# Cross attention and quantised FFN on one core: exponentials head by head from the score bank, a written-out start, and both barriers rebuilt

## Chip, cores, metric

One Trainium2 chip, one of its cores. The metric is the device time of one execution in microseconds; less is better. Times of a kernel come from several runs, and one further execution is profiled.

## What is computed

Eight batches of 512 rows with 512 columns. The first half is a cross attention against 77 context rows per batch with 8 heads, the second half an FFN with activations and weights rounded to 8-bit integers, where the activation's scale comes from the maximum of the whole tensor.

```python
x = x + _L0_xattn_ref(_layernorm(x), ctx_768, Wq, Wk, Wv, Wo, bo)
x = x + _L0_ffn_ref(_layernorm(x), clip_x, clip_down, w_gate, w_up, w_down)

# attention
attn = jnp.einsum('bhsd,bhld->bhsl', q, k) * scale
attn = jax.nn.softmax(attn, axis=-1)
out = jnp.einsum('bhsl,bhld->bhsd', attn, v)

# FFN
def _act_fake_quant(x, clip_factor):
    scale = jax.nn.sigmoid(clip_factor) * jnp.max(jnp.abs(x)) / QMAX
    return jnp.clip(_ste_round(x / scale), -QMAX - 1.0, QMAX) * scale
xq = _act_fake_quant(x, clip_x[0])
gate = xq @ wq(w_gate).T ; up = xq @ wq(w_up).T
h = _act_fake_quant(silu(gate) * up, clip_down[0])
return h @ wq(w_down).T
```

(The last four lines are shortened; wq stands for the weights' rounding, one scale per row.)

## The kernel before

Every instruction is recorded by hand into one queue per engine (class Chain, lines 6 to 60): `add(engine, fn, waits, sig)` appends an instruction that waits for the tokens in `waits` and counts up the semaphore `sig`. Each engine runs its queue strictly in the order in which the Python code calls `add`; nothing else sets the order. PE is TensorE, DVE VectorE, ACT ScalarE, POOL GpSimd; DMAs are issued from SP.

The 4096 rows are 32 row tiles of 128, four per batch. PSUM has QO (two banks, for products of queries, values and attention outputs), SP (two banks, the scores of one row tile: heads 0 to 3 in one, 4 to 7 in the other), PTP (two banks, transposed probabilities), WOP and MI (output products). Products of fp32 precision are three matmuls on a high and a low half: `xT_hi`, `xT_lo` and the like are the splits, one copy on ACT and one subtraction on DVE or POOL.

Per row tile n the attention does: `S(n)`, the score product (line 464), into SP; `soft_max(n)`, a maximum per head on DVE (477); `soft_sub(n)`, scores minus maximum into SBUF, on DVE (484); `soft_exp(n)`, one exponential over all 616 values on ACT, its scale being the row's layer norm factor `r8` (488); `soft_sum`, `soft_rec` on DVE (494, 497); `soft_norm` on POOL (505); `PT(n)`, transposes on PE (517), and `PT_high`, `PT_low`, which copy them out on ACT and DVE. `S(n)` may overwrite the bank once the subtraction of tile n-1 has read it: its waiting list names `t_sub.get(n - 1)`. Per batch come four `q_chunk(b, m)` (the queries, twelve matmuls each, copied out by ACT), `PV_rest` and four `PV` (probabilities times values, 552 to 562, copied out through `os_` by ACT and DVE), and per tile `wo(n)`, the output product (582 to 584, twelve matmuls). `residual`, `second_stats`, `second_scale`, `normed` and `largest` make the second layer norm and its maximum; `w_load` to `w_integer` round one weight tile per step.

`attend(s)` writes out step s. It treats tile s's transposes and tile s+1's scores, in four forms by t = s % 4, and the first batch has exceptions of its own in it. On PE a step with t=0 ends with `PT(s)`, `S(s+1)`; t=1 is `q_chunk`, `S(s+1)`, `wo`, `PT(s)`; t=2 is `S(s+1)`, two `q_chunk`, `wo`, `PT(s)`; t=3 is `S(s+1)`, `wo`, `PT(s)`, `q_chunk`. Ahead of the loop stand value row products `v_rows(0)` to `(2)`, the others lie in the first steps. `last_batch()` writes out steps 28 to 31, where S(30) uses QO and S(31) waits for tile 29.

Between the halves stands the first barrier, `whole_scale(0, ...)` (lines 1053 to 1069): the maximum of all rows of the normed tensor per partition, a transpose on PE to one partition, maximum, scale and reciprocal on 1x1, a second product that spreads both over the partitions, and a copy. `keep_clock(n)` puts n idle products of 128x128 into PE's queue. Then the four row tiles of batch 0 are quantised (`quant_y`, `quant_top`, `quant_low`), transposed on PE (`turn`), and `ffn(b, ic)` runs 88 chunks: four matmuls of gate, four of up, `silu` on ACT, product and maximum on DVE (1133 to 1146). The second barrier has the same form, and the down product follows (1240).

## Time and profile before

| | us |
|---|---|
| median of 3 runs | 553.39 (549.96 to 554.64) |
| profiled execution | 549.97 |
| its span, first to last instruction | 548.1 |
| PE busy | 531.5 (97%) |
| DVE busy | 473.7 (86%) |
| ACT busy | 294.8 (54%) |
| POOL busy | 231.3 (42%) |

The span is what the profile's rows cover; 1.9 us of the execution lie outside it. A busy share is an average over stages: the attention runs to about 300 us, the first half of the FFN to about 463, the down product to the end. Matmuls overlap, and their ends are modelled, so PE's rows are read by the distance of their starts.

### The profile page before, as it was taken

The page shows a single profiled execution, that of the slowest core. Times are in us where ns is not written, and L with a number is a line of the kernel's source. Part 1 is how long each engine was busy: PE and PEld are TensorE (multiplying, and loading weights), DVE is VectorE, ACT ScalarE, POOL GpSimd, SP SyncE. Part 2 cuts the span into 40 slices and gives each one's busy share as a digit, 9 for nine tenths or more (in the row PEclk, how much of TensorE's full clock was granted, in tenths as well). Part 3 has the DMA queues.
Part 4 walks back from the last instruction along what each step waited for, and adds up shares of the span by engine and source line. Part 5 has one row for each costly group of instructions (what it writes and reads, how often), then busy time and mean ns, then how long its engine had stood idle before and what let it go on. Part 6 is the DMA issues. An engine that isn't in the chain of part 4 may idle for free.

```text
span 548.1 us, 8031 instructions
## 1 busy us (share of the span) xinstructions
PE 531.5 (97%) x2704; PEld 357.9 (65%) x2704; DVE 473.7 (86%) x876; ACT 294.8 (54%) x414; POOL 231.3 (42%) x349
## 2 busy tenths in 40 slices
PE   8989889999999999999998799999999999999997
PEld 8868678887888878788777544444444445544444
DVE  4966888989989899898988599999999988899884
ACT  4834646556555654554443555555545533999500
POOL 4386749679596886856544000000000000055442
PEclk9999999999999999999999899999999999999999
DMA  8718365756668565435969917750442220399987
GB/s 310 277 45 304 104 187 180 249 181 192 209 206 252 171 224 185 154 101 182 202 99 329 269 33 293 273 145 24 117 115 46 70 39 15 121 327 229 149 107 129
DMA packets 82658, 93.82 MB, mean 171 GB/s; under 512 B 46801, under 2 KB 49873, under 8 KB 82361
## 3 DMA queue, kind: packets, MB, share of 16 engines
q1 hardware_dynamic: 77593, 84.13, 49.8%
q0 software_dynamic: 4320, 7.87, 9.6%
q10 hardware_dynamic: 704, 1.31, 0.8%
q8 instruction: 21, 0.34, 0.3%
q14 instruction: 20, 0.16, 0.1%
HBM read 47.51 MB, written 37.78 MB: 156 GB/s over the span
## 4 chain that ended last, share of the span: by engine, by line
PE 78%; DVE 11%; SPq 4%; DMA 2%; issue 2%; ACT 1%; POOL 0%; DVEq 0%; POOLq 0%
PE QO L1133 14%; PE SP L1133 14%; PE QO L193 5%; PE QO L195 5%; PE QO L194 5%; PE SP L464 4%; PE PTP L1240 3%; PE QO L1240 3%; PE SP L1240 3%; SPq L41 2%; SPq L37 2%; PE MI L584 2%; PE MI L583 2%; PE MI L582 2%; PE WOP L1240 2%
## 5 line engine op out<-in xcount | busy, mean ns | idle before, releaser
L45 POOL DMA_DIRECT2D out<-n2b x30 | 30.3, 1044 | 210.5 <-DVE n2b L1273 210.5
L1139 ACT ACTIVATE sil<-QO,fsc 128x512 f32<-128x512 f32 x88 | 60.5, 687 | 72.3 <-PE QO L1133 72.3
L1133 PE MATMUL QO<-nT,wgu 128*128 128x512 bf16 x352 | 90.3, 379 | 0.6 <-ACT nT L220 0.6
L1133 PE MATMUL SP<-nT,wgu 128*128 128x512 bf16 x352 | 90.3, 379 | 0.0
L1143 DVE SCALAR_TENSOR_TENSOR h<-SP,fsc,sil 128x512 f32<-128x512 f32 x88 | 65.9, 749 | 9.9 <-PE SP L1133 9.9
L505 POOL TENSOR_TENSOR PN<-P,rs 128x512 f32<-128x512 f32 x64 | 44.2, 712 | 50.3 <-DVE rs L497 50.3
L1146 DVE TENSOR_REDUCE hmx<-h 128x1 f32<-128x512 f32 x88 | 60.4, 686 | 3.0
L1133 PEld LDWEIGHTS QO<-nT,wgu 128*128 128x128 bf16 x352 | 34.4, 98 | 42.0 <-ACT nT L220 0.7
L1133 PEld LDWEIGHTS SP<-nT,wgu 128*128 128x128 bf16 x352 | 34.4, 98 | 41.5
L488 ACT ACTIVATE P<-P,r 128x616 f32<-128x616 f32 x32 | 26.0, 811 | 63.4 <-DVE P L484 63.4
L193 PE MATMUL QO<-xTs,wqs 128*128 128x512 f32 x124 | 50.4, 406 | 2.0 <-DVE xTs L224 1.7
L1207 ACT ACTIVATE h<-h,magic,g 128x1536 f32<-128x1536 f32 (+2 forms) x38 | 47.8, 1350 | 3.7 <-DVE g L221 3.7
L195 PE MATMUL QO<-xTs,wqs 128*128 128x512 f32 x124 | 48.5, 391 | 0.0
L194 PE MATMUL QO<-xTs,wqs 128*128 128x512 f32 x124 | 48.4, 390 | 0.0
L464 PE MATMUL SP<-kst,qs 128*128 128x154 f32 x248 | 38.1, 296 | 3.6 <-DVE P L484 1.8
L603 POOL TENSOR_TENSOR xn<-xn,bob 128x512 f32<-128x512 f32 x32 | 41.2, 1292 | 0.0
L679 ACT ACTIVATE wraw<-wraw,magic,wiv 128x512 f32<-128x512 f32 (+1 forms) x26 | 24.1, 929 | 30.6 <-DVE wiv L672 30.6
L464 PEld LDWEIGHTS SP<-kst,qs 128*128 128x128 f32 x248 | 34.5, 190 | 5.4 <-DVE P L484 2.2
L632 ACT ACTIVATE n<-x,mr,r 128x512 f32<-128x512 f32 x32 | 25.8, 808 | 17.3 <-POOL mr L626 17.3
L1210 DVE TENSOR_SCALAR wgu<-h 128x1536 bf16<-128x1536 f32 (+2 forms) x39 | 29.4, 757 | 1.2 <-ACT h L1207 0.7
L193 PEld LDWEIGHTS QO<-xTs,wqs 128*128 128x128 f32 x124 | 23.2, 187 | 7.5 <-issue 2.2
L494 DVE TENSOR_REDUCE sm<-P 128x8 f32<-128x616 f32 x32 | 25.2, 786 | 2.6 <-ACT P L488 1.7
(207 smaller groups left out, 1193.6 us busy)
## 6 DMA issues: line engine op xcount, KB each, us to landing
xTr<-in_xT SPq DMA_DIRECT2D x8, 1024.0 KB, 7.5
xn<-in_x SPq DMA_DIRECT2D x32, 256.0 KB, 3.9
out<-x SPq DMA_DIRECT2D x32, 256.0 KB, 2.9
n_rows<-n SPq DMA_DIRECT2D x32, 256.0 KB, 2.7
n2b<-n_rows SPq DMA_DIRECT2D x32, 256.0 KB, 3.8
out<-n2b POOLq DMA_DIRECT2D x30, 256.0 KB, 5.9
h_spill<-h SPq DMA_DIRECT2D x2, 2816.0 KB, 9.9
h<-h_spill SPq DMA_DIRECT2D x6, 768.0 KB, 7.1
```

What stands on the lines that cost most here:

```text
L193: e.matmul(ps, lh, rh, start=(i == 0), stop=False)
L194: e.matmul(ps, lh, rl, start=False, stop=False)
L195: m = e.matmul(ps, ll, rh, start=False, stop=(i == n - 1))
L464: m = e.matmul(o, qs[:, b % 2, j, w], kst[:, b, j, :], start=(j % 2 == 0), stop=True, skip_group_check=True)
L505: t_norm[n] = add("pool", lambda e, to=to, rb=rb, l0=l0, l1=l1: e.tensor_tensor(to, u[:, :, l0:l1], rb, ALU.mult), [t_rec[n], t_PT.get(n - ...
L603: t_xb[n] = add("pool", lambda e: e.tensor_tensor(xn[:, n % XR, :], xn[:, n % XR, :], bob[:, :], ALU.add), [t_bn1[n], t_bo], "xb")
L1133: m = e.matmul(ps, wv_[:, k, col:col + 128], nT[:, b % 2, :, k, :], start=(k == 0), stop=(k == 3))
L1139: t_sil[n] = add("act", lambda e: e.activation(sil[:, n % SR, :], gp, ACT.Silu, scale=fsc[:, ic:ic + 1]), [t_g[n], t_fs, t_h.get(n - SR)] ...
L1143: t_h[n] = add("dve", lambda e: e.scalar_tensor_tensor(out=hv, in0=up, scalar=fsc[:, 11 + ic:12 + ic], in1=sil[:, n % SR, :], op0=ALU.mult ...
L1146: t_hm[n] = add("dve", lambda e: e.tensor_reduce(hmx[:, n:n + 1], hv, AX.X, ALU.max, apply_absolute_value=True), [t_h[n]], "hmx")
L1207: a = add("act", lambda e: e.activation(hv, hv, ACT.Identity, bias=magic[:, :], scale=g2[:, 1, 1:2]), [t_g2] + ([t_back[b, p]] if b < 2 el ...
L1240: mm = e.matmul(ps, hq[:, i % 2, k, tt * 128:tt * 128 + 128], wd[:, k, :], start=(k == 0), stop=(k == NI - 1))
```

## The change

1. Softmax. `soft_sub` and `soft_sum` go. `soft_shift(n)` makes, from the maxima and `r8`, a bias of 128x8. `soft_exp(n)` is eight activations, one per head, that read 77 columns of the score bank with that bias and `r8` as scale, write the exponentials to SBUF and their sum through `accum_out`. Everything that waited for `t_sub` to reuse a score bank now waits for `t_exp`.
2. The first four tiles and the product of batch 0 with its values are written out in one list ahead of the loop; value row products are split into `v_mm` and `v_out` and stand between the score products. `attend` begins at step 4 and loses its exceptions. PV of batch 0 uses MI and WOP instead of SP.
3. Barriers. The column of maxima scales an identity matrix (DVE), one product with ones spreads it over all partitions, and scale and reciprocal are made on 128 partitions; the second product and the copy go. The keep-clock counts are 14 and 7, 6 and 8 (8, 4 and 10 before). The last row tile is normed on DVE (`last_normed`); the Silu table is loaded ahead of it.
4. First FFN product. Rows of batch 0 are transposed tile by tile, and `first_rows(tt)` computes chunks 0 and 1 for 128 rows at a time. `last_chunk` does the last chunk in two halves. At the down product the first clip stands directly behind its rounding.

```diff
-        def v_rows(r):
+        v_at = {}
+
+        def v_mm(r):
...
-            last = qo_product(pairs, 512, m, [t_wvl, t_ctxl], lambda bank: [
-                (bank, vst[0:m, r % 2, 0, :], vst[0:m, r % 2, 1, :])], [t_v.get(r - 2)])
-            t_v[r] = dma("sp", vd[r * 128:r * 128 + m], vst[0:m, r % 2], list(last), f"st_v{r % 2}")
+            v_at[r] = qo_bank(pairs, 512, m, [t_wvl, t_ctxl])
+
+        def v_out(r):
+            m = min(128, NB * L - r * 128)
+            at, bank, t = v_at[r]
+            hi, lo = vst[0:m, r % 2, 0, :], vst[0:m, r % 2, 1, :]
+            th = add("act", lambda e: e.activation(hi, bank, ACT.Copy), [t, t_v.get(r - 2)], "qo_hi")
+            tl = add("dve", lambda e: e.tensor_tensor(lo, bank, hi.bitcast(f32), ALU.subtract),
+                     [th, t_v.get(r - 2)], "qo_lo")
+            state["free"][at] = (tl,)
+            t_v[r] = dma("sp", vd[r * 128:r * 128 + m], vst[0:m, r % 2], [th, tl], f"st_v{r % 2}")
...
             else:
-                free = [t_sub[29] if n == 31 else t_sub.get(n - 1)]
-            if t == 1 and b > 0:
+                free = [t_exp[29] if n == 31 else t_exp.get(n - 1)]
+            if t == 1 and b > 1:
                 free += [t_oss[b - 1, 2], t_oss[b - 1, 3]]
 
...
-        def soft_sub(n):
-            u = P[:, n % UR, 0:HL].rearrange("p (a h l) -> p a h l", a=2, h=4)
-            mb = mx8[:, n % 2, :].rearrange("p (a h) -> p a h", a=2).unsqueeze(3).broadcast_to(
-                [128, 2, 4, L])
-            t_sub[n] = add("dve", lambda e: e.tensor_tensor(u, S4(n), mb, ALU.subtract),
-                           [t_mx[n], t_norm.get(n - UR), t_wkl, t_ctxl], "sm_sub")
+        def soft_shift(n):
+
+            t_sub[n] = add("dve", lambda e: e.tensor_scalar(nb8[:, n % 2, :], mx8[:, n % 2, :], r8[:, n:n + 1], -1.0,
+                                                            ALU.mult, ALU.mult),
+                           [t_mx[n], t_r8[n], t_exp.get(n - 2)], "sm_sub")
 
         def soft_exp(n):
-            t_exp[n] = add("act", lambda e: e.activation(P[:, n % UR, 0:HL], P[:, n % UR, 0:HL], ACT.Exp,
-                                                         scale=r8[:, n:n + 1]),
-                           [t_sub[n], t_r8[n]], "sm_exp")
-
-        def soft_sum(n):
-            u = P[:, n % UR, 0:HL].rearrange("p (h l) -> p h l", h=H)
-            t_sum[n] = add("dve", lambda e: e.reduce_sum(sm8[:, n % 2, :], u, AX.X), [t_exp[n]], "sm_sum")
+
+            for hh in range(H):
+                at = (hh // 4) * 512 + (hh % 4) * L
+                t_exp[n] = add("act", lambda e, hh=hh, at=at: e.activation(
+                    P[:, n % UR, hh * L:hh * L + L], S_bank(n)[:, at:at + L], ACT.Exp, bias=nb8[:, n % 2, hh:hh + 1],
+                    scale=r8[:, n:n + 1], accum_out=sm8[:, n % 2, hh:hh + 1]),
+                               [t_sub[n], t_norm.get(n - UR), t_rec.get(n - 2), t_wkl, t_ctxl], "sm_exp")
 
...
-                           [t_sum[n], t_norm.get(n - 2)], "sm_rec")
+                           [t_exp[n], t_norm.get(n - 2)], "sm_rec")
...
-            banks = []
+            banks = [] if b else [(None, MI[:, :], ()), (None, WOP[:, :], (t_c,))]
...
+            if b:
+                for k in range(2):
+                    banks.append((None, SP[:, 512 * k:512 * k + 512], (t_exp[min(4 * b + 4, NT - 1)],)))
             pv_at[b] = banks
 
...
+        def last_normed(n):
+
+            k = n % RR
+            t_n2[n] = add("dve", lambda e: e.tensor_scalar(n2[:, k, :], x1[:, k, :], mv2[:, n, 0:1], r2[:, n:n + 1],
+                                                           ALU.subtract, ALU.mult),
+                          [t_r2[n], t_n2s[n - RR], t_am[n - RR]], "n2_d")
+            t_n2s[n] = dma("sp", n2d[n], n2[:, k, :], [t_n2[n]], f"st_n2_{k}")
...
+        w_load(0)
+        w_load(1)
+
+        v_mm(0)
+        S(0)
+        soft(0, "max", "sub")
+        v_out(0)
+        soft(0, "exp")
+        split_lo(1, 0, "dve")
+        v_mm(1)
+        v_out(1)
+        load_vb(0)
+        v_mm(2)
+        S(1)
+        first_bias(0)
+        soft(0, "rec", "norm")
+        split_lo(1, 2, "dve")
+        t_xT[2] = load_xT(2, t_xTs[1])
+        v_out(2)
+        soft(1, "max", "sub", "exp")
+        v_mm(3)
+        v_out(3)
+        PT(0)
+        q_chunk(1, 0)
+        PT_high(0)
+        PT_low(0)
+        first_bias(1)
+        soft(1, "rec", "norm")
+        S(2)
+        soft(2, "max", "sub", "exp")
+        row_stats(3)
+        q_chunk(1, 1)
+        PT(1)
+        PT_high(1)
+        PT_low(1)
+        soft(2, "rec", "norm")
+        S(3)
+        soft(3, "max", "sub", "exp")
+        v_mm(4)
+        w_tops(0)
+        v_out(4)
...
+        first_bias(2)
+        q_chunk(1, 2)
+        PT(2)
+        soft(3, "rec", "norm")
+        PT_high(2)
+        PT_low(2)
+        w_round(0)
+        w_integer(0)
+        w_load(2)
+        row_stats(4)
+        first_bias(3)
+        w_tops(1)
+        w_round(1)
+        w_integer(1)
+        w_load(3)
+        PT(3)
+        PT_high(3)
+        PT_low(3)
+        row_stats(5)
+        q_chunk(1, 3)
+        for k in range(4):
+            split_hi(2, k)
+        split_lo(2, 0)
+        split_lo(2, 1)
+        S(4)
+        t_flat = [t_v[4], t_v[3], t_wol, ("qo_mm", c.count["qo_mm"])]
+        split_lo(2, 2, "dve")
+        soft(4, "max", "sub", "exp")
+        split_lo(2, 3, "dve")
+        PV_rest(0)
+        PV(0, 2)
+        PV(0, 3)
+        PV(0, 0)
+        PV(0, 1)
+        soft(4, "rec", "norm")
+        first_bias(4)
+        q_chunk(2, 0)
+        w_tops(2)
+        w_round(2)
+        w_integer(2)
+        row_stats(6)
+        first_bias(5)
+        first_bias(6)
 
         DEFER = (1, 2)
 
...
+                S(s + 1)
+                soft_max(s + 1)
+                soft_shift(s + 1)
+                load_vb(b)
                 PT_high(s)
-                if s > 0:
-                    soft_exp(s + 1)
+                soft_exp(s + 1)
                 if t not in DEFER:
...
-            if n < 31:
-                largest(2 * n - 32)
-                largest(2 * n - 31)
+            for at in {28: (24, 25), 29: (26, 27), 30: (28,), 31: (29, 30)}[n]:
+                largest(at)
             if n == 30:
                 load_n2(0, gone + [t_n2s[tt] for tt in range(4)])
-        largest(30)
-        normed(31)
+        add("act", lambda e: e.activation(warm[:, :], sge[0:1, :], ACT.Silu), [t_sge], "warm")
+        last_normed(31)
         largest(31)
...
+        def whole_scale(which, src, diag, diag_waits, waits, ahead, behind):
+
+            keep_clock(ahead)
+            a = add("dve", lambda e: e.tensor_reduce(gcol[:, which:which + 1], src, AX.X, ALU.max), waits,
+                    "g_col")
+            a = add("dve", lambda e: e.tensor_scalar_mul(diag, identF[:, :], gcol[:, which:which + 1]),
+                    [a, *diag_waits], "g_dg")
+            a = add("pe", lambda e: e.matmul(MI[:, 0:128], ones[:, :], diag, start=True, stop=True),
+                    [a], "g_mm")
+            keep_clock(behind)
+            a = add("dve", lambda e: e.reduce_max(gtop[:, which:which + 1], MI[:, 0:128], AX.X), [a],
+                    "g_top")
+            a = add("dve", lambda e: e.tensor_scalar(g2[:, which, 0:1], gtop[:, which:which + 1],
                                                      sg[:, which:which + 1], 1.0 / 127.0, ALU.mult,
-                                                     ALU.mult), [a, t_sg], "g_s")
-            a = add("dve", lambda e: e.reciprocal(gsc[:, which, 1:2], gsc[:, which, 0:1]), [a], "g_s")
-            a = add("pe", lambda e: e.matmul(MI[:, 256:258], ones[0:1, :], gsc[:, which, :],
-                                             start=True, stop=True), [a], "g_mm")
-            keep_clock(10)
-            return copy("dve", g2[:, which, :], MI[:, 256:258], [a], "g_out")
-
-
-        t_g1 = whole_scale(0, amx[:, :], [("amx", c.count["amx"])])
+                                                     ALU.mult), [a, t_sg], "g_out")
+            return add("dve", lambda e: e.reciprocal(g2[:, which, 1:2], g2[:, which, 0:1]), [a], "g_out")
+
+
+        t_g1 = whole_scale(0, amx[:, :], wraw[:, 1, 0:128], [t_wb[25], t_ws[25]],
+                           [("amx", c.count["amx"])], 14, 7)
...
+        def last_chunk():
+
+            n, b, ic = NB * NI - 1, NB - 1, NI - 1
+            wv_ = wgu[:, :].rearrange("p (k n) -> p k n", k=4)
+            for half in range(2):
+                w = slice(half * 256, half * 256 + 256)
+                at = (n % 2) * 512
+                gp = QO[:, at:at + 256] if half else PTP[:, 0:256]
+                up = SP[:, at:at + 256] if half else PTP[:, 512:768]
...
+        def first_rows(tt):
+
+            wv_ = wgu[:, :].rearrange("p (k n) -> p k n", k=4)
+            w = slice(tt * 128, tt * 128 + 128)
+            for ic in range(2):
+                for bank, col, into in ((QO, ic * 128, t_g), (SP, I + ic * 128, t_u)):
+                    def fn(e, bank=bank, col=col, ic=ic):
+                        for k in range(4):
+                            m = e.matmul(bank[:, ic * 512:ic * 512 + 512][:, w], wv_[:, k, col:col + 128],
+                                         nT[:, 0, tt, k, :], start=(k == 0), stop=(k == 3))
+                        return m
+                    into[ic] = add("pe", fn, [t_nT[tt], t_wgu, t_sdb], "g_mm1" if into is t_g else "u_mm")
...
-        for tt in (0, 2, 1, 3):
+        for tt in (0, 1, 2):
             quant_y(0, tt)
-        for tt in (0, 1):
+        for tt in (0, 1, 2):
             quant_top(0, tt)
-        for tt in (0, 1):
             quant_low(0, tt)
-        for tt in (2, 3):
-            quant_top(0, tt)
-        for tt in (2, 3):
-            quant_low(0, tt)
+        turn(0, 0, "act")
+        turn(0, 1, "dve")
+        first_rows(0)
+        quant_y(0, 3)
+        turn(0, 2, "act")
+        first_rows(1)
+        quant_top(0, 3)
+        quant_low(0, 3)
         t_fs = add("dve", lambda e: e.tensor_scalar_mul(fsc[:, :], wsc[:, 0:22], g2[:, 0, 0:1]),
                    [t_g1], "fsc")
-        for tt in range(4):
-            turn(0, tt, "dve" if tt == 3 else "act")
+        turn(0, 3, "dve")
+        first_rows(2)
+        first_rows(3)
         for b in range(NB):
             for ic in range(NI):
+                if (b, ic) == (NB - 1, NI - 1):
+                    last_chunk()
+                    continue
...
+                at = (0, 1, 3, 4) if b == 0 else (0, 2, 4, 6)
+                if b + 1 < NB and ic in at:
+                    tt = at.index(ic)
...
-        t_g2 = whole_scale(1, hmx[:, :], [("hmx", c.count["hmx"])])
+        t_g2 = whole_scale(1, hmx[:, :], bob[:, 0:128], [t_am[31]], [("hmx", c.count["hmx"])], 6, 8)
...
             if p == 0:
+                finish_h()
+            if p == 3:
                 t_sds = add("dve", lambda e: e.tensor_scalar_mul(sdb[:, :], sdb[:, :], g2[:, 1, 0:1]),
                             [t_g2, t_sdb], "sds")
```

How the queues change where the prediction looks. ACT in a batch of the attention, from the copies of PV's outputs (`os`) on; `pts` is PT_high, `qs` a query chunk, P the exponentials, wraw the weight rounding. Before:

```order
L566 ACTIVATE os<-QO 128x512 [waits qo_mm] x2
L220 ACTIVATE pts<-PTP 128x5x128 [waits PT]
L488 ACTIVATE P<-P,r 128x616 [waits r8,sm_sub]
L220 ACTIVATE qs<-QO 128x512 [waits qo_mm]
L488 ACTIVATE P<-P,r 128x616 [waits r8,sm_sub]
L679 ACTIVATE wraw<-wraw,magic,wiv 128x1408 [waits w_iv]
```

After:

```order
L576 ACTIVATE os<-QO 128x512 [waits qo_mm] x2
L220 ACTIVATE pts<-PTP 128x5x128 [waits PT]
L500 ACTIVATE P,sm<-SP,nb,r 128x77 [waits sm_rec,sm_nrm,sm_sub]
L500 ACTIVATE P,sm<-SP,nb,r 128x77 x7
L220 ACTIVATE qs<-QO 128x512 [waits qo_mm]
L500 ACTIVATE P,sm<-SP,nb,r 128x77 [waits sm_rec,sm_nrm,sm_sub]
L500 ACTIVATE P,sm<-SP,nb,r 128x77 x7
L697 ACTIVATE wraw<-wraw,magic,wiv 128x1408 [waits w_iv]
```

The order is the same; each exponential has become eight, and they read SP instead of P.

ACT over the first four tiles, from tile 0's exponential to tile 3's; `vst` is the copy of a value row product, `xTs` a split of x. Before:

```order
L488 ACTIVATE P<-P,r8 128x616
L210 ACTIVATE vst<-QO 128x512 x2
L488 ACTIVATE P<-P,r8 128x616
L730 ACTIVATE sge<-clips 1x2
L220 ACTIVATE pts<-PTP 128x5x128
L210 ACTIVATE vst<-QO 128x512
L220 ACTIVATE qs<-QO 128x512
L488 ACTIVATE P<-P,r8 128x616
L220 ACTIVATE qs<-QO 128x512
L679 ACTIVATE wraw<-wraw,magic,wiv 128x512
L220 ACTIVATE pts<-PTP 128x5x128
L488 ACTIVATE P<-P,r8 128x616
```

After:

```order
L500 ACTIVATE P,sm8<-SP,nb8,r8 128x77 x8
L398 ACTIVATE vst<-QO 128x512 x2
L500 ACTIVATE P,sm8<-SP,nb8,r8 128x77 x8
L398 ACTIVATE vst<-QO 128x512
L220 ACTIVATE qs<-QO 128x512
L220 ACTIVATE pts<-PTP 128x5x128
L500 ACTIVATE P,sm8<-SP,nb8,r8 128x77 x8
L220 ACTIVATE qs<-QO 128x512
L220 ACTIVATE pts<-PTP 128x5x128
L500 ACTIVATE P,sm8<-SP,nb8,r8 128x77 x8
L398 ACTIVATE vst<-QO 104x512
```

One query chunk and one PT_high now stand between neighbouring exponentials, and the last value row's copy comes behind those of tile 3.

DVE at the first barrier, from the last norm's maxima on; `gcol`, `gtop`, `gsc` and `g2` are the maxima and scales, `n2b` and `qb` the rows quantised. Before:

```order
L638 TENSOR_REDUCE amx<-n2 128x1 x2
L1057 TENSOR_REDUCE gcol<-amx 128x1
L1061 TENSOR_REDUCE gtop<-MI 1x1
L1063 TENSOR_SCALAR gsc<-gtop,sg 1x1
L1066 RECIPROCAL gsc<-gsc 1x1
L221 COPY g2<-MI 128x2
L1087 TENSOR_SCALAR n2b<-n2b,g2 128x512 x2
L1095 TENSOR_SCALAR qb<-n2b 128x512 x2
L1101 TENSOR_SCALAR qb<-qb 128x512 x2
```

After:

```order
L655 TENSOR_SCALAR n2<-x1,mv2,r2 128x512
L648 TENSOR_REDUCE amx<-n2 128x1
L1107 TENSOR_REDUCE gcol<-amx 128x1
L1109 TENSOR_SCALAR wraw<-identF,gcol 128x128
L1114 TENSOR_REDUCE gtop<-MI 128x1
L1116 TENSOR_SCALAR g2<-gtop,sg 128x1
L1119 RECIPROCAL g2<-g2 128x1
L1137 TENSOR_SCALAR n2b<-n2b,g2 128x512
L1145 TENSOR_SCALAR qb<-n2b 128x512
L1151 TENSOR_SCALAR qb<-qb 128x512
```

The norm has come to DVE, the copy from PE's second product is gone, and tile 0's rounding and clip stand directly behind its scaling.

## Rows read from the trace of the kernel before

**Rows 1.** The page, busy time of an engine (us, share of the span, instructions).
```profile
PE 531.5 (97%) x2704; PEld 357.9 (65%) x2704; DVE 473.7 (86%) x876; ACT 294.8 (54%) x414; POOL 231.3 (42%) x349
```

**Rows 2.** One batch by windows: length, busy PE PEld DVE ACT POOL, clock, DMA share, GB/s.
```profile
105.50:138.20 32.70, 32.41 (x175) 26.96 (x173) 30.31 (x62) 18.84 (x29) 24.43 (x40) 1.00 0.67 209
```

**Rows 3.** Chain that ended last, score products: start, length, what (PE SP L464).
```profile
105.69 1.05 PE SP L464 x8
...
109.48 1.05 PE SP L464 x8
...
113.85 1.05 PE SP L464 x8
...
240.09 1.05 PE SP L464 x8
...
244.45 1.05 PE SP L464 x8
```

**Rows 4.** Timeline, one tile's softmax: start us, length us, instruction [idle before <-releaser].
```profile
107.01 0.79 DVE L477 TENSOR_REDUCE mx<-SP 128x8 f32<-128x616 f32 x1
107.84 0.80 DVE L484 TENSOR_TENSOR P<-SP,mx 128x616 f32<-128x616 f32 x1
...
108.67 0.81 ACT L488 ACTIVATE P<-P,r 128x616 f32<-128x616 f32 x1 [2.24 <-DVE P L484]
```

**Rows 5.** Timeline of ACT: neighbouring activations (total length of x) and the smallest one.
```profile
122.39 2.17 ACT L220 ACTIVATE xTs<-xTr 128x512 fp32r<-128x512 f32 x4
...
290.78 1.27 ACT L1014 ACTIVATE wraw<-identF,wsc 128x128 f32<-128x128 f32 x4
...
304.00 0.20 ACT L1044 ACTIVATE warm<-sge 1x2 f32<-1x2 f32 x1
305.68 1.52 ACT L1090 ACTIVATE n2b<-n2b,magic,g 128x512 f32<-128x512 f32 x2 [1.48 <-DVE g L221]
```

**Rows 6.** Timeline of PE: score products S(0), S(1) and S(5).
```profile
32.47 1.21 PE L464 MATMUL SP<-kst,qs 128*128 128x154 f32 x8
...
37.58 1.19 PE L464 MATMUL SP<-kst,qs 128*128 128x154 f32 x7 [1.80 <-DVE P L484]
...
72.94 1.29 PE L464 MATMUL SP<-kst,qs 128*128 128x154 f32 x8 [1.57 <-DVE os L567]
```

**Rows 7.** Timeline of PE in the last batch: S(31) and PT(31).
```profile
271.25 1.21 PE L464 MATMUL SP<-kst,qs 128*128 128x154 f32 x8
...
278.93 0.71 PE L517 MATMUL PTP<-identF,PN 128*128 128x128 f32 x5
```

**Rows 8.** Timeline of PE: first matmul of a query chunk at t=3, behind PT at 127.25.
```profile
128.25 0.47 PE L193 MATMUL QO<-xTs,wqs 128*128 128x512 f32 x1 [0.28 <-DVE xTs L224]
```

**Rows 9.** First barrier: timeline of PE and DVE, and one window (columns as in rows 2).
```profile
303.20 0.27 PE L1058 MATMUL MI<-identF,gcol 128*1 128x128 f32 x1 [3.18 <-DVE gcol L1057]
...
305.43 0.16 DVE L221 COPY g<-MI 128x2 f32<-128x2 f32 x1 [1.22 <-PE MI L1067]
...
308.49 0.61 PE L1109 MATMUL PTP<-identB,qb 128*128 128x128 bf16 x8
...
311.09 1.02 PE L1133 MATMUL QO<-nT,wgu 128*128 128x512 bf16 x4 [0.56 <-ACT nT L220]
...
305.00:307.00 2.00, 2.00 (x10) 1.99 (x11) 1.47 (x5) 1.32 (x2) 0.00 (x0) 0.50 0.87 257
```

**Rows 10.** Second barrier: timeline of DVE and PE, scale to first down product.
```profile
466.55 0.16 DVE L221 COPY g<-MI 128x2 f32<-128x2 f32 x1 [0.50 <-PE MI L1067]
466.74 0.49 DVE L1204 TENSOR_SCALAR h<-h,g 128x512 f32<-128x512 f32 x1
467.26 0.43 DVE L1210 TENSOR_SCALAR wgu<-h 128x512 bf16<-128x512 f32 x1
...
468.34 0.29 DVE L1221 TENSOR_SCALAR wgu<-wgu 128x512 bf16<-128x512 bf16 x1
...
468.77 0.59 PE L1240 MATMUL QO<-wd,wgu 128*128 128x512 bf16 x2
```

214 lines of the change are left out of this document (82 added, 132 removed).

## The prediction, made before the changed kernel was run

> **What bounds the kernel now.** I read the page's busy shares first. TensorE (PE) is at work for 531.5 of 548.1 us [rows 1]. A matmul's end is modelled, so 97% alone proves little; the table by stretches and the chain of waits decide. Over one batch of the attention (four row tiles, 105.5 to 138.2) PE works 32.41 of 32.70 us, DVE 30.31, ACT 18.84 [rows 2]: DVE is nearly full, ACT has 14 us free, and PE has no hole. The chain says the same: from one score product to the next it holds nothing but PE instructions, 3.79 us from the first score product of a batch's group to the second, 4.37 us to the third (4.36 in the last such batch) [rows 3]. So in the attention only PE's time counts. Work taken off DVE is worth nothing there, and a wait put into PE's queue is paid in full, because PE's instructions run in order and the products behind the waiting one wait too. The reader should carry one thing from this view: the free time of this stage is ACT's and its critical resource is PE's order. The holes that exist lie in the first four tiles, and at the two barriers.
>
> **Part A, the softmax in the steady state (tiles 5 to 28).** Before, per tile: DVE maximum 0.79 us and subtraction 0.80 us [rows 4], then ACT one exponential over 616 elements, 0.81 us [rows 4], then a DVE sum and reciprocal. The subtraction frees the score bank, so the next score product waits only for maximum and subtraction: from 107.01 the bank is free at 108.64, and PE comes back to it at 109.48 [rows 3, 4]. After, the subtraction and the sum go from DVE, a shift of 128x8 elements comes (I take 0.18 us, of the kind of the small DVE steps at the barrier, 0.16 in [rows 9]), and ACT does eight exponentials that read the score bank. The bank is free only when the eighth has ended: the waiting list of S names t_exp where it named t_sub.
>
> What does one head's exponential cost? The trace of before has no activation of 77 columns with two per-partition operands and an accumulator. Its neighbours: four identities of 128x128 with one such operand take 1.27 us together and 0.387 each, so a new one starts every 0.295 [rows 5]; 51 columns fewer at 0.83 ns is 0.04 less. Two of 128x512 with two operands take 1.52 us, 0.80 each: one starts every 0.72; four copies of 128x512 without operands take 2.17 us, one every 0.52 [rows 5], so two operands cost 0.2. That gives 0.35 us between starts if the accumulator is free. It is the lower end. The accumulator's result has to be written after the data. If that ends the overlap of neighbours (0.09 us), a head costs its whole length, 0.44, say 0.45. If it is also an instruction of its own, as long as the smallest activation here, 0.20 [rows 5], a head costs 0.65: the upper end. I take 0.45, nearest to the rows' whole lengths; eight are 3.6 us, where one was 0.81.
>
> The Trainium skill ("VectorE: DVE Perf Modes", section on the TRN2 errata) speaks against this change: every ScalarE instruction pays a fixed cost, so small tiles should be avoided; its table gives 172 cycles plus one per element at 1.2 GHz from PSUM, by which a head would take an estimated 0.21 us. The trace agrees with the fixed cost (0.387 us for 128 columns [rows 5]) but its row is dearer than the table, since the row has a per-partition operand. By the table alone the waits of part A would be 1.7 us in all; that result is a rival below.
>
> Chain from the start of a score product to the next one allowed: 1.05 us of product and 0.2 until the maximum starts, maximum 0.79, shift 0.2, hand-over and eight heads 3.65, release 0.06: 5.95 us. PE comes back after 3.79: it waits 2.15. From the second to the third product: 5.95 against 4.37, wait 1.6. From the third on there are two query chunks and an output product between, no wait. 3.75 us a batch, six batches: **+22.4**. With 0.35 a head it is 1.35 + 0.8 = 2.15 a batch, +13; with 0.65, 3.75 + 3.2, +42. ACT's load rises from 18.8 by 4 x (3.6 - 0.8) to 30 us a batch of now 36: not the bound. DVE's falls by some 6 us, which nobody waits for, but for one small PE wait a batch: query chunk 0 of the batch after next waits for a DVE split, 0.28 us in the timeline and 0.45 from start to start [rows 8]; five of these may go, **-2**.
>
> **Part B, the last batch.** S(31) waits for exponential 29 (t_sub[29] before). It started at 271.25 with nothing idle before it [rows 7], two score products and an output product (some 5.05 us) behind the start of S(29), whose bank it takes. The chain is 5.95: wait 0.9. Exponentials 29, 30 and 31 now stand one behind the other on ACT (10.8 us with a norm between) and PT(31), which ran at 278.93 [rows 7], needs tile 31's norm on POOL, near 281.7: another 1.9 on top. **+2.8** (0.6 to 7 at the two ends).
>
> **Part C, the first four tiles.** Before, S(0) starts at 32.47, and PE waits 1.80 us ahead of S(1) and 1.57 ahead of S(5) at 72.94 [rows 6]; with two waits of 0.9 and small gaps between, I count some 7 us in that view. The written order puts query chunks (twelve matmuls, 3.79 - 1.05 = 2.74 us [rows 3], so 0.23 each) and value products (nine, 2.1 us) between score products. But each score product now waits 5.95 us behind the previous one, more where DVE or ACT has something ahead. Walked through in the order shown (start, what it waits for): S(0) 32.5; two value products; S(1) 38.4, heads of tile 0, wait 0.8; value product 3, its bank freed late, 0.3; transposes, chunk (1,0); S(2) 46.2, wait 1.0; its bank again, 0.3; chunk (1,1); S(3) 53.4, wait 2.6, since PT_low(0) and the reciprocal stand before maximum 2 on DVE; value product 4, chunk (1,2); PT(3) 63.0, wait 3.2, since v_out(4) on ACT and DVE stands ahead of the reciprocal of tile 3, whose heads end at 60.1; chunk (1,3), S(4); PV; chunk (2,0) 75.2, wait 4.4, since the copies that free its bank stand behind the heads of tile 4, and these behind four splits, on ACT. The waits are 12.6 against 7: **+5.6**, S(5) near 78.5. With heads at 0.35 it is +2.4, at 0.65 +12. Here the change's aim, filling, is beaten by its own longer chain. A longer idle PE may also lower its clock: before, idle 3.18 us at the first barrier was followed by a granted clock of 0.50, that is 1.2 GHz [rows 9]; idle 1.80 was not. This could add 1 to 3 us and stays in the range.
>
> **Part D, the first barrier and the first FFN product.** Before: the maximum goes through one transpose, a 1x1 scale, a second product to spread it (DVE idle 1.22 us before the copy at 305.43), the first transposes of quantised rows start at 308.49 behind ten keep-clock products, and the FFN at 311.09 [rows 9]. After: one product of ones with a diagonal spreads the maxima at once; 1.22 + 0.16 go, 0.2 of diagonal come: -1.2. The last norm moves from ACT (0.80 for such an operation [rows 5]) to DVE (0.49 [rows 10]), -0.3. The first transposes started 2.9 us after the scale; with y, top and low of tile 0 directly one behind the other (0.49 + 0.43 + 0.29 [rows 10]) and seven keep-clock products it is 1.25: -1.65. From there to the end of chunks 0 and 1 (sixteen matmuls of 512 columns at some 0.22 us behind 311.09, so 314.5) it was 6.05, with products tile by tile as they come it is about 4.7: -1.35. **-4.5**, between -2 (if DVE, which takes over the pace of the FFN's chunks, cannot use all of it) and -5.
>
> **Part E, the second barrier.** The same spreading saves DVE's idle 0.50 and its copy 0.16 but adds 0.2 [rows 10]. The last chunk in halves shortens silu, product and maximum by 0.2. The first down product started 2.06 us after the scale at 466.71 [rows 10]; with the second clip directly behind it 1.3. **-1.4** (-0.5 to -2).
>
> Sum: 22.4 - 2 + 2.8 + 5.6 - 4.5 - 1.4 = **+22.9** on the profiled execution's 549.97, 572.9. The median of the three runs shown, 553.39, lies 3.4 above that execution, which is at the low end of the three (549.96); I add half of it: 575.
>
> **At nothing.** The clips read on 128 partitions and the weight loads and load_vb(0) issued earlier on SP: DMAs with slack behind four tiles of PE work, and POOL's bias additions are only shifted in its queue; if one of these came late it would cost about one PE wait of part C, 1 to 2 us. The Silu table is loaded before the last norm instead of behind it, beside DVE's statistics. The waits for the row stores move from the quantisation to batch 4; no row shows that they were last. residual's engine argument is never used.
>
> **Rivals.**
> - Accumulator free (0.35 a head). For it: neighbouring activations overlap in every row here. 13 - 2 + 0.6 + 2.4 - 5.9 = +8: 559.6. Chance 0.2. With an error of 5 us it reaches into no change.
> - Accumulator read as its own instruction without overlap (0.65): 42 + 7 + 12 - 8 = +53: 604. Chance 0.12.
> - Faster: a head costs at most 0.21 us. Then the chain is 4.0 us, PE waits 0.3 once a batch (+1.7), the first tiles lose 4.5 of their 7 us of holes, and with -2 and -5.9 it is 10.7 less: 541. It decides at about 0.17 to 0.2 a head (3.79 - 2.3 = 1.5 us for eight). Against it stand all rows of [rows 5]. It is what the Trainium skill's table would give. Chance 0.1.
> - The change doesn't do what it says: the S wait is on t_exp but other waits on PE hide it. Nothing in [rows 3] is idle that could hide it; inside 1% (547.9 to 558.9) together with the low tail of the first rival: 0.12.
>
> **Numbers.** Forecast case 0.46; with rivals 0.2, 0.12, 0.1 and 0.12. About 1% is what a measurement of this kernel can tell from no change. Faster by over 1%: 0.11; within 1%: 0.12; slower by over 1%: 0.77. The range is 553 to 600: below lies the fast rival and part of the unchanged ones, above most of the dearest.
>
> **What would show it.** In the profile after: a group of 256 activations of 128x77; their start-to-start in the timeline is the number on which all hangs (right: 0.40 to 0.50). PE idle before score products, released by ACT, two a batch, 2.2 and 1.6 us; a batch takes 36 instead of 32.7 us; ACT's busy time up by 80 to 95 us, DVE's down by 45. S(5) after 75 us. The stretch from the last score row's residual to the FFN shorter by 4 to 5 us. I am wrong if PE shows no idle before the score products of a batch, or if a head costs under 0.25 us.

## The result, and the profile after

| | before | after |
|---|---|---|
| median of the runs, us | 553.39 | 586.65 (586.21, 590.88, 586.65) |
| ratio, 95% interval | 1 | 1.064 (1.058 to 1.071) |
| profiled execution, its span | 549.97, 548.1 | 586.21, 584.4 |

The changed kernel is slower by 33 us by the medians and by 36.2 by the profiled executions, against which the terms were priced. The forecast was slower, 575, from a sum of +22.9.

The page after, first lines, to be held against [rows 1]: busy us, share of the span, instructions.

```profile
PE 542.9 (93%) x2740; PEld 364.1 (62%) x2740; DVE 440.3 (75%) x847; ACT 372.1 (64%) x894; POOL 233.0 (40%) x349
...
PE 48%; DVE 19%; ACT 18%; POOL 6%; issue 5%; DMA 2%; SPq 0%; ACTq 0%; DVEq 0%; POOLq 0%
ACT P L500 14%; PE SP L1183 12%; PE QO L1183 12%; PE QO L1340 3%; PE PTP L1340 3%; PE SP L1340 3%; PE SP L474 3%; DVE mx L487 3%; POOL xTs L224 2%; DVE nb L492 2%; DVE os L577 2%; DVE bn L624 2%; PE QO L193 2%; PE QO L195 2%; PE WOP L1340 2%
```

DVE lost 33 us of work and ACT got 77 more (45 and 80 to 95 in the forecast), and no engine is full. The chain of waits, which held only PE between the score products of a batch before [rows 3], now runs through the exponentials (ACT P L500, 14% of the span, 82 us). A page where the two busiest engines have become freer and the time has grown is the sign of a serial chain.

The waits of the whole run name it: engine, line, what it waited for, us, times, longest.

```profile
DVE rs L506 <- ACT P L500: 50.5, 27, 3.0
PEld SP L474 <- ACT P L500: 26.1, 16, 2.5
PE SP L474 <- ACT P L500: 20.6, 16, 2.2
```

Before, no score product waited for ACT in that list; now 16 do.

Where the 36.2 us arose, by marks read from the two timelines (S(n) is the score product of tile n; the differences are of unrounded times):

| stretch | before | after | difference | forecast |
|---|---|---|---|---|
| start to S(5) | 72.9 | 81.5 | +8.6 | +5.6 |
| S(5) to S(29) | 193.2 | 222.1 | +28.8 | +20.4 |
| S(29) to the end of the last residual | 33.0 | 34.8 | +1.8 | +2.8 |
| to the 44th maximum of the FFN (88 in all) | 89.6 | 87.3 | -2.3 | -4.5 |
| to the first down product | 80.0 | 79.2 | -0.8 | -1.4 |
| to the end | 79.4 | 79.4 | 0 | 0 |

**One batch.** Windows, columns as in [rows 2], then PE's timeline of its score products (start, length, idle before and its releaser).

```profile
118.00:155.60 37.60, 34.37 (x174) 28.06 (x174) 26.66 (x58) 28.61 (x89) 24.93 (x40) 0.95 0.57 180
```

```profile
117.83 1.22 PE L474 MATMUL SP<-kst,qs 128*128 128x154 f32 x8
...
123.75 1.34 PE L474 MATMUL SP<-kst,qs 128*128 128x154 f32 x8 [1.96 <-ACT P L500]
...
130.63 1.32 PE L474 MATMUL SP<-kst,qs 128*128 128x154 f32 x8 [0.67 <-ACT P L500]
...
140.53 1.22 PE L474 MATMUL SP<-kst,qs 128*128 128x154 f32 x8
...
155.41 1.22 PE L474 MATMUL SP<-kst,qs 128*128 128x154 f32 x8
```

The batch takes 37.6 us, 4.9 more than the 32.7 of [rows 2]. The four distances were 3.8, 4.4, 9.8 and 14.7 us; they are 5.9, 6.9, 9.9 and 14.9. So +2.1 and +2.5 lie at the two products that follow one another closely, and +0.3 in the rest (a new wait of 0.75 ahead of the product of the probabilities with the values, and about 0.45 less at the query chunk of [rows 8]).

**The head.** ACT's timeline of the first tile of that batch, first three heads and the end.

```profile
120.40 0.42 ACT L500 ACTIVATE P<-SP,nb,r 128x77 f32<-128x77 f32 x1 [1.67 <-DVE nb L492]
120.72 0.19 ACT L500 ACTIVATION_READ_ACCUMULATOR P<-SP,nb,r 128x1 f32 x1
120.81 0.40 ACT L500 ACTIVATE P<-SP,nb,r 128x77 f32<-128x77 f32 x1
121.11 0.19 ACT L500 ACTIVATION_READ_ACCUMULATOR P<-SP,nb,r 128x1 f32 x1
121.21 0.41 ACT L500 ACTIVATE P<-SP,nb,r 128x77 f32<-128x77 f32 x1
...
123.17 0.43 ACT L500 ACTIVATE P<-SP,nb,r 128x77 f32<-128x77 f32 x1
123.47 0.22 ACT L500 ACTIVATION_READ_ACCUMULATOR P<-SP,nb,r 128x1 f32 x1
```

A head is two instructions. The read of the accumulator is 0.2 us long, but it starts 0.1 before its exponential's row ends, and the next head 0.1 before the read's row ends: from head to head 0.39 (median of the 256). Eight take 3.3 us, not the 3.6 of the forecast.

**The shift.** The next tile, DVE's timeline and then POOL's.

```profile
125.12 0.80 DVE L487 TENSOR_REDUCE mx<-SP 128x8 f32<-128x616 f32 x1 [1.20 <-PE SP L474]
125.96 1.29 DVE L492 TENSOR_SCALAR nb<-mx,r 128x8 f32<-128x8 f32 x1
127.16 0.67 DVE L648 TENSOR_REDUCE amx<-n 128x1 f32<-128x512 f32 x1
```

```profile
124.01 1.38 POOL L514 TENSOR_TENSOR PN<-P,rs 128x512 f32<-128x512 f32 x2 [5.57 <-DVE rs L506]
125.36 0.62 POOL L703 TENSOR_SCALAR wint<-wraw 128x512 bf16<-128x512 f32 x1
125.94 1.28 POOL L613 TENSOR_TENSOR xn<-xn,bob 128x512 f32<-128x512 f32 x1
```

The shift of eight columns takes 0.22 to 0.25 us in 22 of the 32 tiles, near the estimate, but here 1.29, and it ends (127.25) just behind POOL's addition of the bias (127.22). This comes once in each of five batches, from the third on, and in some of the first tiles. It lengthens the chain from the second to the third score product.

**PE's clock.** Windows; the granted clock is the third column from the end.

```profile
125.00:128.00 3.00, 3.00 (x9) 2.32 (x8) 2.84 (x4) 0.72 (x4) 2.22 (x4) 0.50 0.05 11
...
53.30:56.50 3.20, 3.19 (x11) 2.92 (x12) 1.66 (x3) 1.04 (x2) 1.11 (x2) 0.50 1.02 358
...
77.00:80.30 3.30, 3.30 (x10) 2.61 (x9) 3.20 (x10) 0.23 (x1) 1.83 (x3) 0.52 0.03 7
```

It falls to 0.50 (1.2 GHz) behind PE's idle of 1.96 us in the batches, of 2.24 ahead of S(3), and of 3.85 ahead of query chunk (2,0). While it is low, the output product's matmuls start 0.43 us apart instead of 0.23.

**The tail.** PE's timeline at the first barrier and DVE's at the second, to be held against [rows 9, 10].

```profile
342.52 0.49 PE L1111 MATMUL MI<-wraw,ones 128*128 128x128 f32 x2 [1.03 <-DVE wraw L1109]
...
345.22 0.40 PE L1159 MATMUL PTP<-identB,qb 128*128 128x128 bf16 x4 [0.65 <-DVE qb L1151]
345.89 0.40 PE L1159 MATMUL PTP<-identB,qb 128*128 128x128 bf16 x4 [0.27 <-DVE qb L1151]
346.31 0.40 PE L1235 MATMUL QO<-nT,wgu 128*128 128x128 bf16 x4
...
350.12 0.39 PE L1235 MATMUL SP<-nT,wgu 128*128 128x128 bf16 x4
```

```profile
502.85 0.29 DVE L1114 TENSOR_REDUCE gtop<-MI 128x1 f32<-128x128 f32 x1 [0.58 <-PE MI L1111]
503.18 0.21 DVE L1116 TENSOR_SCALAR g<-gtop,sg 128x1 f32<-128x1 f32 x1
503.43 0.16 DVE L1119 RECIPROCAL g<-g 128x1 f32<-128x1 f32 x1
503.63 0.49 DVE L1304 TENSOR_SCALAR h<-h,g 128x512 f32<-128x512 f32 x1
```

From the last residual's end to the first transposes of quantised rows it is 6.83 us instead of 9.35. The first silu starts 11.5 us behind the residual instead of 13.0, the third FFN maximum ends only 1.0 us earlier than before, the 44th 2.3.

### The profile page after: what moved, and what is told of

It reads as the page before. It is cut to its first block, busy times and chain, and to the rows that moved or that the text cites. A ratio compares the mean times of both kernels' runs of the same rounds, so it can differ in the third digit from the quotient of the medians.

```text
span 584.4 us, 8579 instructions
## 1 busy us (share of the span) xinstructions
PE 542.9 (93%) x2740; PEld 364.1 (62%) x2740; DVE 440.3 (75%) x847; ACT 372.1 (64%) x894; POOL 233.0 (40%) x349
## 4 chain that ended last, share of the span: by engine, by line
PE 48%; DVE 19%; ACT 18%; POOL 6%; issue 5%; DMA 2%; SPq 0%; ACTq 0%; DVEq 0%; POOLq 0%
ACT P L500 14%; PE SP L1183 12%; PE QO L1183 12%; PE QO L1340 3%; PE PTP L1340 3%; PE SP L1340 3%; PE SP L474 3%; DVE mx L487 3%; POOL xTs L224 2%; DVE nb L492 2%; DVE os L577 2%; DVE bn L624 2%; PE QO L193 2%; PE QO L195 2%; PE WOP L1340 2%
## 5 line engine op out<-in xcount | busy, mean ns | idle before, releaser
L500 ACT ACTIVATE P<-SP,nb,r 128x77 f32<-128x77 f32 x248 | 99.2, 420 | 54.4 <-DVE nb L492 54.3
L1183 PE MATMUL SP<-nT,wgu 128*128 128x512 bf16 x340 | 87.3, 379 | 0.4
L1183 PE MATMUL QO<-nT,wgu 128*128 128x512 bf16 x340 | 87.3, 379 | 0.1
L474 PE MATMUL SP<-kst,qs 128*128 128x154 f32 x248 | 41.1, 310 | 21.3 <-ACT P L500 20.6
L1183 PEld LDWEIGHTS SP<-nT,wgu 128*128 128x128 bf16 x340 | 32.9, 98 | 41.4 <-DVE h L1194 2.5
L1183 PEld LDWEIGHTS QO<-nT,wgu 128*128 128x128 bf16 x340 | 33.2, 98 | 40.2 <-ACT sil L1190 0.3
L193 PE MATMUL QO<-xTs,wqs 128*128 128x512 f32 x124 | 51.3, 414 | 3.8 <-DVE os L577 3.8
L474 PEld LDWEIGHTS SP<-kst,qs 128*128 128x128 f32 x248 | 34.8, 194 | 27.5 <-ACT P L500 26.1
L500 ACT ACTIVATION_READ_ACCUMULATOR P<-SP,nb,r 128x1 f32 x248 | 51.5, 207 | 0.0
L195 PE MATMUL QO<-xTs,wqs 128*128 128x512 f32 x124 | 49.2, 396 | 0.0
L194 PE MATMUL QO<-xTs,wqs 128*128 128x512 f32 x124 | 48.8, 394 | 0.0
L506 DVE RECIPROCAL rs<-sm 128x8 f32<-128x8 f32 x32 | 6.5, 202 | 50.5 <-ACT P L500 50.5
L487 DVE TENSOR_REDUCE mx<-SP 128x8 f32<-128x616 f32 x31 | 24.4, 788 | 14.8 <-PE SP L474 14.8
```

Of the source, the lines that this page charges most:

```text
L193: e.matmul(ps, lh, rh, start=(i == 0), stop=False)
L194: e.matmul(ps, lh, rl, start=False, stop=False)
L195: m = e.matmul(ps, ll, rh, start=False, stop=(i == n - 1))
L474: m = e.matmul(o, qs[:, b % 2, j, w], kst[:, b, j, :], start=(j % 2 == 0), stop=True, skip_group_check=True)
L500: t_exp[n] = add("act", lambda e, hh=hh, at=at: e.activation(P[:, n % UR, hh * L:hh * L + L], S_bank(n)[:, at:at + L], ACT.Exp, bias=nb8[: ...
L1183: m = e.matmul(ps, wv_[:, k, col:col + 128], nT[:, b % 2, :, k, :], start=(k == 0), stop=(k == 3))
```

## The experiments

"Theory" is at first the forecast's: the price is the time for which the exponentials hold the score bank. Each kernel was timed beside runs of the kernel before on the same chip (medians 550.9 to 551.9 there); ratios are to those.

### 1. The changed kernel with the softmax of before

```diff
-                free = [t_exp[29] if n == 31 else t_exp.get(n - 1)]
+                free = [t_sub[29] if n == 31 else t_sub.get(n - 1)]
...
-            t_sub[n] = add("dve", lambda e: e.tensor_scalar(nb8[:, n % 2, :], mx8[:, n % 2, :], r8[:, n:n + 1], -1.0,
+            t_sub[n] = add("dve", lambda e: e.tensor_tensor(u, S4(n), mb, ALU.subtract),
```

(with the one exponential and the DVE sum of before)

> The changed kernel with the softmax of before (maximum, subtraction, one exponential, sum) and the score bank free after the subtraction again; written start, barriers and FFN product stay. Theory: the loss is the score bank's longer hold alone. Then a batch takes 32.7 us again (37.6 in the changed kernel), the last batch gives back 1.9, and the first tiles at least the 8.6 us they lost (S(5) at 73 or earlier): 586.7 - 28.8 - 1.9 - 9 = 547, a few us faster than before. Rival: the written order of the first tiles and the other moves cost part of it themselves; then S(5) stays at 78 or later and the time is 552 or more.

Measured: 554.1 us, ratio 1.005 (1.004 to 1.007). 32 us of the loss are gone, so the head-by-head softmax is what costs. But this kernel isn't faster than before, although its tail is: S(5) is at 76.8 where it was at 72.9, and a batch takes 33.2 instead of 32.7. By its time the rival's side of the expectation came true, though S(5) lies between the two; runs 2 and 10 sort it out.

### 2. The kernel before with the exponentials head by head

```diff
-            t_sub[n] = add("dve", lambda e: e.tensor_tensor(u, S4(n), mb, ALU.subtract),
+            t_sub[n] = add("dve", lambda e: e.tensor_scalar(nb8[:, n % 2, :], mx8[:, n % 2, :], r8[:, n:n + 1], -1.0,
...
+            for hh in range(H):
+                at = (hh // 4) * 512 + (hh % 4) * L
```

> The kernel before with only the head-by-head exponentials from the score bank (shift, eight exponentials with accumulator, bank free after the eighth). Theory: this part alone costs 28.8 in the steady batches, 1.9 in the last one and 4 to 9 in the first tiles: 553.4 + 37 = 590, slower than the changed kernel by what its barriers and FFN product give (3 us). Rival: the order of the changed kernel is what makes the wait; then the time is under 575.

Measured: 591.6, ratio 1.072 (1.069 to 1.075): as the theory has it. Windows of one batch:

```profile
120.40:157.90 37.50, 34.29 (x174) 28.13 (x173) 26.31 (x58) 28.53 (x89) 24.83 (x40) 0.95 0.58 182
```

The batch has the 37.5 us of the changed kernel, in the order of before. S(5) is at 84.2, 11.2 later than before; with heads the written start (81.5) gives back 2.6 us of that.

### 3. Sums by DVE, no accumulator

```diff
-                    scale=r8[:, n:n + 1], accum_out=sm8[:, n % 2, hh:hh + 1]),
+                    scale=r8[:, n:n + 1]),
...
         def soft_rec(n):
+            soft_sum(n)
```

> The changed kernel without the accumulator: the eight exponentials only write, and DVE sums the 616 elements before the reciprocal (0.7 us more on DVE a tile). In the changed kernel a head starts every 0.40 us and leaves an accumulator read of 0.2 us that overlaps the next head. Theory: the read costs 0.1 a head (the identities without accumulator start every 0.295): a head every 0.31, a tile's chain 0.7 shorter, two waits a batch 0.7 shorter each, six batches and the first tiles: 586.7 - 8.4 - 2 = 576. Rival: the read is hidden, the spacing is set by the exponential itself and stays 0.40: 587 or more, since DVE has 0.7 a tile more.

Measured: 577.6, ratio 1.044 (1.037 to 1.051). ACT's timeline of one tile:

```profile
122.32 2.56 ACT L500 ACTIVATE P<-SP,nb,r 128x77 f32<-128x77 f32 x8 [1.67 <-DVE nb L492]
```

A head starts every 0.300 us (median), so the accumulator costs 0.093 a head and 0.7 a tile. The whole run is 9 us faster and a batch takes 35.6, 2.0 less, but that isn't the accumulator's alone. The second score product follows the first after 5.19 us instead of 5.92, as the head's price says; the third follows after 5.15 instead of 6.88, which is 1.0 more than that price. The shift of this tile takes 0.31 us here, because POOL's addition no longer runs beside it. So two heads' prices make 1.5 us a batch and the shift 1.0, and 0.4 is lost again in the rest of the batch.

### 4. The shift in a two-input form

```diff
-e.tensor_scalar(nb8[:, n % 2, :], mx8[:, n % 2, :], r8[:, n:n + 1], -1.0, ALU.mult, ALU.mult)
+e.scalar_tensor_tensor(out=nb8[:, n % 2, :], in0=mx8[:, n % 2, :], scalar=-1.0,
+    in1=r8[:, n:n + 1].broadcast_to([128, H]), op0=ALU.mult, op1=ALU.mult)
```

> The changed kernel with the shift as a scalar_tensor_tensor (two inputs, one of them the scale spread over eight columns) instead of a tensor_scalar; same result, same place. In the changed kernel the shift takes 0.22 us, but 1.12 to 1.29 in the second tile of each batch and ends there with a GpSimd addition that runs beside it. Theory: the single-input form is held up while GpSimd uses the memory, the two-input form is not. Then all shifts take 0.20 to 0.25, the third score product of a batch comes 1.0 us earlier, a batch takes 36.6: 586.7 - 6.3 - 1 = 579. Rival: any small DVE operation waits there (or the GpSimd operation only looks late); then 1.1 to 1.3 us stay and the time is 586.

Measured: 585.1, ratio 1.061 (1.058 to 1.064). The rival. DVE's and POOL's rows at the same place:

```profile
126.73 1.32 DVE L492 SCALAR_TENSOR_TENSOR nb<-mx,r 128x8 f32<-128x8 f32 x1
```

```profile
126.73 1.29 POOL L614 TENSOR_TENSOR xn<-xn,bob 128x512 f32<-128x512 f32 x1
```

Elsewhere this form takes 0.15 to 0.17 us; beside the addition it waits just as long. The run settles something else: the clock. Its batch, by windows:

```profile
118.70:156.10 37.40, 32.72 (x174) 26.86 (x173) 26.47 (x58) 28.53 (x89) 24.81 (x40) 1.00 0.56 180
```

The clock stayed at 1.00 here and PE was busy 32.7 instead of 34.4 us, yet the batch takes 37.4 against 37.6. PE waits 2.28 us for the third product instead of 0.67. The half clock of the changed kernel's batches thus lies inside the wait ahead of that product and costs 0.2 us a batch at most. That holds for this order of PE; run 8 has another.

### 5. The tail alone, on the kernel before

```diff
-            a = add("pe", lambda e: e.transpose(MI[0:1, 0:128], gcol[:, which:which + 1], identF[:, :]),
+            a = add("pe", lambda e: e.matmul(MI[:, 0:128], ones[:, :], diag, start=True, stop=True),
...
+                if (b, ic) == (NB - 1, NI - 1):
+                    last_chunk()
```

(with last_normed, first_rows, and the other edits behind the attention)

> The kernel before with only the changed tail: both barriers through the diagonal product, the last norm on DVE, the first FFN product by row tiles, the last chunk in halves. By the prediction these give 4.5 and 1.4: 547.5. By the trace of the changed kernel (stretch from the last residual to the 44th FFN maximum 2.3 us shorter, last FFN maximum to first down product 0.8 shorter) they give 3.1: 550.3.

Measured: 546.8 (546.1 to 548.7), ratio 0.992 (0.989 to 0.995), faster than both kernels. That is between 3.0 and 5.9 us. By the traces it is 3.1: 2.3 by the 44th FFN maximum, as in the changed kernel, and 0.6 at the second barrier, where the changed kernel has 0.8.

### 6. POOL's addition of the next tile moved

```diff
             when("s", soft_norm, s + 1)
+            if t == 2:
+                when("x", first_bias, s + 2)
...
-                when("x", first_bias, s + 3)
+                if t != 1:
+                    when("x", first_bias, s + 3)
```

> The changed kernel with one GpSimd operation of the second tile of each batch, the addition of the bias to 128x512 of x, issued one tile later, behind the next norm. With either form of the shift, the shift of that tile ended 0.02 us behind this addition. Theory: a DVE operation from SBUF that starts beside such a GpSimd addition waits until it ends; moved away, the shift there takes 0.23 us (1.12 to 1.29 in the changed kernel), the third score product of a batch comes 1.0 earlier and a batch takes 36.6: 580.5. Rival: the shift waits for something else and stays above 1 us: 586.7.

Measured: 591.6, ratio 1.072 (1.066 to 1.077). The aim was missed: the addition that runs beside the shift comes from step t = 0, and this moved the one of t = 1. The shift still took 0.7 to 1.3 us, and both waits stayed. The way from the fourth score product to the next batch grew from 14.9 to 15.5 us, so that a batch took 38.1; by which wait isn't shown. Run 9 moves the right one.

### 7. The bank freed by DVE, eight exponentials from the copy

```diff
+            t_sub[n] = add("dve", lambda e: e.tensor_tensor(u, S4(n), mb, ALU.subtract),
...
-                    P[:, n % UR, hh * L:hh * L + L], S_bank(n)[:, at:at + L], ACT.Exp, bias=nb8[:, n % 2, hh:hh + 1],
+                    P[:, n % UR, hh * L:hh * L + L], P[:, n % UR, hh * L:hh * L + L], ACT.Exp,
...
-                free = [t_exp[29] if n == 31 else t_exp.get(n - 1)]
+                free = [t_sub[29] if n == 31 else t_sub.get(n - 1)]
```

> The changed kernel, where DVE's subtraction (0.8 us) copies the scores out of the bank as before and frees it, and the eight exponentials with accumulator read the copy. ACT has the same eight instructions, PE's bank is free early. Theory: the price is the bank's hold. Then no wait ahead of score products, a batch takes 33 to 33.5 and the time is 586.7 - 25 - 2 - 4 = 556. Rival: the length of the softmax itself (the probabilities come 2.1 us later than with one exponential) holds up the transposes and output products; then a batch stays at 35 or more and the time is over 568.

Measured: 572.0, ratio 1.036 (1.031 to 1.041), on the rival's side. The score products:

```profile
116.54 1.29 PE L474 MATMUL SP<-kst,qs 128*128 128x154 f32 x8 [0.97 <-DVE os L577]
...
120.44 1.21 PE L474 MATMUL SP<-kst,qs 128*128 128x154 f32 x8
...
124.97 1.22 PE L474 MATMUL SP<-kst,qs 128*128 128x154 f32 x8
```

The two waits for the bank are gone (distances 3.9 and 4.5, as before), but a batch takes 35.4. The other 2.7 us have spread over waits of 0.3 to 1.1 ahead of score products, query chunks, transposes and the product with the values. So freeing the bank early is worth 14.7 us of the changed kernel's loss. (Two more things differ: the subtraction of 0.8 us is back on DVE in place of the shift, and a head, which reads the copy and has one per-row operand less, starts every 0.343 us instead of 0.393.) This kernel differs from run 10 (552.2) only in eight exponentials and accumulator reads for one exponential and a DVE sum, and the difference is 19.7: ACT's length costs even where it holds no bank, because the copies that free PE's other banks stand behind the heads in ACT's queue. That last reason is read from the queue's order and the next run; it was not tried by itself.

### 8. PE's order spread

```diff
                 if t == 1 and b + 1 < NB:
-                    q_chunk(b + 1, t)
+                    q_chunk(b + 1, 1)
+                    q_chunk(b + 1, 2)
+                if t == 2 and b + 1 < NB:
+                    q_chunk(b + 1, 3)
                 when("s", S, s + 1)
...
             else:
+                when("wo", wo, s - 5)
                 when("s", S, s + 1)
```

> The changed kernel with PE's order in the steady batches spread: query chunk 2 ahead of the second score product, chunk 3 ahead of the third, the output product of the fourth tile ahead of the fourth, so that score products stand 6.5, 7.1, 7.2 and 11.9 us apart instead of 3.8, 4.4, 9.8 and 14.7. Softmax, ACT and bank as in the changed kernel. Theory: the wait is the chain of 5.9 (6.9 where the shift is held up) less PE's own distance; it goes to 0, a batch takes 33.4 and the time is 562. Rival: copies of the query chunks on ACT, now before and behind the heads, hold PE up instead; then a batch takes over 35.5 and the time is over 574.

Measured: 586.0, ratio 1.061 (1.056 to 1.067): no gain at all. The score products wait no more, but the loss stands elsewhere. PE, then DVE, at the end of the third tile's step:

```profile
140.73 1.21 PE L474 MATMUL SP<-kst,qs 128*128 128x154 f32 x8
144.61 0.74 PE L526 MATMUL PTP<-identF,PN 128*128 128x128 f32 x5 [2.67 <-DVE pts L224]
```

```profile
143.64 0.82 DVE L224 TENSOR_TENSOR pts<-PTP,pts 128x640 fp32r<-128x640 f32 x1 [0.85 <-ACT pts L220]
144.38 0.91 DVE L492 TENSOR_SCALAR nb<-mx,r 128x8 f32<-128x8 f32 x1
```

The transposes wait 2.67 us for the low half of the previous tile's probabilities (DVE), this for the high half (ACT, 142.93 to 143.61), and that stands on ACT behind the rounding of a weight and four splits, which follow the last tile's heads (these end at 139.7). A batch takes 37.7, 5.0 more than before. By PE's starts 2.7 of it is this wait and 0.4 one ahead of the query chunk behind it. Most of the rest is the clock, by windows:

```profile
146.60:150.00 3.40, 3.40 (x10) 2.63 (x9) 1.97 (x5) 2.60 (x12) 3.05 (x7) 0.50 0.73 228
```

Eight of the query chunk's matmuls start 0.43 us apart instead of 0.23, which is 1.6 us, and no wait behind them takes it up. The distance between score products was thus only the first of two limits; the second, as this chain reads, is ACT's queue as a whole, and the half clock that was hidden in the changed kernel comes on top.

### 9. The right addition moved

```diff
+        def first_bias(n, *waits):
...
                 when("s", soft_exp, s + 1)
+                if t == 1:
+                    first_bias(s + 2, t_sub[s + 1])
```

> The changed kernel with the GpSimd bias addition of the first tile of each batch (the one that really ran beside the held-up shift; the run before moved its neighbour) issued in the next tile with a wait on that tile's shift, so that it runs behind it. Theory: the DVE shift is held up by the GpSimd addition. It then takes 0.23 us (1.12 to 1.29 in the changed kernel) and the third score product of a batch comes 1.0 earlier: batch 36.6, 580.5. Rival: the shift waits for something else, stays above 1 us, 586.7; or the loss only moves, since PE's next wait (0.75 ahead of the output product of the batch) grows by the same: batch 37.4 with a short shift.

Measured: 582.3, ratio 1.055 (1.052 to 1.058). DVE's and POOL's rows of the tile:

```profile
163.51 0.23 DVE L492 TENSOR_SCALAR nb<-mx,r 128x8 f32<-128x8 f32 x1
```

```profile
163.89 1.30 POOL L613 TENSOR_TENSOR xn<-xn,bob 128x512 f32<-128x512 f32 x1 [0.34 <-DVE nb L492]
```

With the addition behind it the shift takes 0.23 us. The third score product follows the second after 5.8 us instead of 6.9, and the batch takes 36.5. In two later batches that distance was 6.8 again, with a clock of 0.76 in the window from 234 to 241, and in an earlier one 6.2, with 0.54 from 125 to 128: with the short shift the half clock is no longer hidden and costs 0.4 to 1 us where it comes.

### 10. Run 1 with the sum in its old places

```diff
-            soft_sum(n)
...
+                when("s", soft_sum, s + 1)
                 when("wo", second_stats, s - 5)
                 when("s", soft_rec, s + 1)
```

> The kernel of the first run (changed kernel, softmax of before) with the DVE sum in the places it has in the kernel before (there it stood directly ahead of the reciprocal, behind the statistics in the fourth tile). The first run's batch took 33.2 us against 32.7. Theory: that was the sum's place; the batch goes back to 32.7, and what remains against the kernel before is the written start (+3.9 at the sixth score product) and the tail (about -4.8): 551.0. Rival: the changed steady order itself costs 0.5 a batch; then 554.

Measured: 552.2 (551.0 to 553.6), ratio 1.001 (1.000 to 1.003). One batch:

```profile
176.60:209.40 32.80, 32.53 (x175) 27.02 (x174) 30.36 (x62) 18.84 (x29) 24.77 (x40) 1.00 0.66 205
```

The batch is that of [rows 2] again, so the changed steady order costs nothing. What remains is the written start, without the heads: S(5) is at 75.1, 2.2 late, S(9) 4.3 late and S(13) 5.7, by waits for splits and transposes in the first two batches; the tail's gain makes up for about half of it. By S(13) the written start is worth 2.5 us with the long softmax (157.9 in run 2, 155.4 in the changed kernel) and costs 5.7 with the short one.

### 11. The tail, and one split of the start later

```diff
-            split_lo(1, k, ("dve", "pool")[k % 2])
+            if k != 2:
+                split_lo(1, k, ("dve", "pool")[k % 2])
...
         soft_sub(0)
+        split_lo(1, 2, "dve")
```

> The kernel before with the changed tail (546.8 in its run), and in the first tiles one DVE split moved from ahead of the first softmax to behind its subtraction. In the trace of before this split took 2.94 us (31.72 to 34.66, its like takes 0.68), beside a GpSimd split that ended at 34.11, and PE waited 1.98 ahead of the second score product. Theory: the second score product comes 1.3 to 1.9 earlier and part of it lasts: 545.8. Rival: the wait is taken over by the next ones in the first tiles (1.07, 1.05 and 1.74 long), the sixth score product stays at 73.3 and the time at 546.8.

Measured: 546.8, ratio 0.991 (0.989 to 0.993): the rival. S(1) came 0.5 earlier, and S(5) stands at 73.6 against 73.3 in run 5. Run 5's kernel stays the fastest that was found.

### 12. The shift in the accumulator form

```diff
-                                                            ALU.mult, ALU.mult),
+                                                            ALU.mult, ALU.mult, accum_out=gsh[:, :]),
```

> The changed kernel with the GpSimd work in its old place and the shift still a tensor_scalar, but in the form that also writes an accumulator (a 128x1 sum that nothing reads). Theory: what holds the shift up is that DVE's plain single-input form and its form with two inputs from SBUF both need a path to memory that the GpSimd addition holds; the form with the accumulator reads one input by its own path. This is the rule of the Trainium skill, page SBUF, State Buffer, section Who interferes with whom. Then every shift takes 0.2 to 0.35 us though the addition still runs beside it, the third score product of a batch comes 1.0 earlier and a batch takes 36.5: 580.5, or up to 2 us more if each of the 32 shifts costs 0.06 more for its accumulator. Rival: any DVE operation of this place waits for the GpSimd addition; then 1.1 to 1.3 us and 586.5.

Measured: 580.1 (579.3 to 581.1), ratio 1.052 (1.049 to 1.054), 0.4 from the expectation. DVE, then POOL:

```profile
198.52 0.22 DVE L493 TENSOR_SCALAR_CACHE_REDUCE nb<-mx,r 128x8 f32<-128x8 f32 x1
198.67 0.08 DVE L493 DVE_READ_ACCUMULATOR nb<-mx,r 128x1 f32 x1
198.67 0.68 DVE L649 TENSOR_REDUCE amx<-n 128x1 f32<-128x512 f32 x1
```

```profile
198.01 1.28 POOL L614 TENSOR_TENSOR xn<-xn,bob 128x512 f32<-128x512 f32 x1
```

The addition had been running for 0.5 us when the shift began, and the shift takes 0.22 us, as all 32 do (mean 0.218). So neither the neighbour alone nor the place decides, but the form. One argument gives 6.6 us by the medians, 5.8 by the profiled executions.

## Why the prediction was right, and where it was not

**Direction and place: right.** The time went where the forecast put it: two waits a batch for the exponentials, ahead of the second and third score product, in a stage where only PE counts. Run 2 makes the loss from that part alone, run 10 takes it away: the heads cost 34.4 us of the changed kernel (586.65 less 552.24). The mechanism is the forecast's only in part: with the bank free early (run 7) 14.7 us of this go, and 19.7 stay.

**Part A, first wait: right.** 2.15 was forecast, 2.1 measured. The head's price (0.45) was somewhat high at 0.39; the bound of 0.65 for an accumulator read as its own instruction had the instruction right and the overlap wrong. What the shorter heads saved, the shift (0.22, not 0.18), the product and the hand-overs between took back (the maximum starts 1.48 us behind the product's start, not 1.25; that was so before too, where PE's timeline has the product of [rows 4] at 105.53): the chain is 5.9 us, as added up.

**Part A, second wait: mis-sized, 1.6 forecast, 2.5 measured.** The step that failed is "shift 0.2". It was priced by its size; in this place it takes 1.29 beside POOL's addition. Runs 9 and 12 show that this is the cause, and what it is worth: in run 12 5.0 us from S(5) to S(29) and 0.8 ahead of S(5).

**Part A, "from the third on no wait": nearly.** A new wait of 0.75 us a batch came ahead of the product with the values, for the copy of a query chunk late in ACT's queue. "The q-chunk wait goes, -2" was right in size, and was more than cancelled by this one. With both, 28.8 us from S(5) to S(29) against 20.4.

**"ACT's load is not the bound": true as a sum, wrong as a reason.** 28.6 of 37.6 us are busy, but the order of ACT's queue seems to bind: run 7 still loses 2.7 us a batch with the bank free early, and run 8, with the score products apart, loses as much at the transposes, 1.6 at the half clock and 0.4 at a query chunk. The forecast had one limit where there are two that lie on top of each other. No run shortens ACT's queue by itself, so the second is read from rows and not shown by a run.

**Part B: +2.8 forecast, +1.8 measured.** Within its bounds; S(31) waits 0.7 us instead of 0.9, and what follows it loses 1.1 instead of 1.9.

**Part C: +5.6 forecast, +8.6 measured.** The waits ahead of the named products were 1.05, 1.02, 2.40, 1.91 and 4.0 us by PE's starts against 0.8, 1.0, 2.6, 3.2 and 4.4 in the walk, and S(4) waited 0.85 where none was seen: 11.3 against 12.6 in all. The "7 us" that the forecast took off for the kernel before was too high as well: read in the same way its waits are 1.97, 1.08, 1.05 and 1.74, 5.8 in all. So the waits grew by 5.5 us where 5.6 was forecast, but by two sums that were each over by 1.2 to 1.3: luck. What was missing is the clock, which the walk had left out of the sum and kept in the range at 1 to 3 us: it is 0.50 in the windows behind S(3) and behind chunk (2,0). From that chunk to S(5) it is 5.0 us where twelve matmuls and five transposes at full clock take 3.4 (2.75 and 0.54, and 0.1 for the first), and the products from 53.3 to 56.7 lose another 1.4: 3.0 us together.

**Part D: -4.5 forecast, -2.3 measured.** The steps up to the first transposes were right in size (2.5 of 3.15). The failed one is "the end of chunks 0 and 1, -1.35": products by row tiles delay the first silu, since they complete all four parts of two chunks together at 350; the silu started 4.65 us behind the first transposes instead of 3.66. By the third maximum 1.0 of 2.5 us is left. PE itself starts chunk 2 12.2 us behind the last residual instead of 15.4, 3.2 earlier where 4.5 was forecast; three waits for banks that DVE frees late, up to chunk 7, take 0.9 of this back, and 2.3 stay. The range's reason (DVE sets the pace there) was the right one.

**Part E: -1.4 forecast, -0.8 measured**, -0.6 in run 5. The down product's start was right: 1.33 us behind the scaling of h instead of 2.03. The spreading was not: from the last maximum of the FFN to that scaling it is 1.96 us instead of 2.04, since DVE now makes the diagonal and then waits 0.58 us for the product ahead of the maximum over it. The last chunk in halves gave nothing that shows: 75.9 us from the 44th maximum to the last against 76.0.

**The rivals.** The free accumulator (0.35 a head) would need what run 3 made by leaving it out, at 0.30 a head. Its two waits are 1.4 and 0.8 us there, as the rival has them; even so the time was 577.6 and not 560, since S(5) came 9.6 us late instead of 2.4 and a batch loses 0.7 beyond the two waits. The faster head of 0.21 us is refuted by each of the 256.

## What to carry to other kernels

A bank that is handed over by a wait is priced by the whole chain that holds it less the distance at which the waiting engine comes back; add every link at its length beside its neighbours, not at its length alone. A long occupation of an engine that has room left by its busy share still delays every small copy behind it in its queue, so moving the waiting product elsewhere may only move the wait. An order written by hand fits one set of durations: the start that gains 2.5 us with one softmax loses 5.7 with another.

## What the runs showed of the hardware that was not expected

- A small DVE operation can wait for the whole of a GpSimd operation that runs beside it, and this depends on its form. Beside POOL's 128x512 addition of 1.28 us the shift took 1.29 us as TENSOR_SCALAR and 1.32 as SCALAR_TENSOR_TENSOR with both inputs in SBUF (0.22 and 0.15 to 0.17 otherwise), but 0.22 as the tensor_scalar that writes an accumulator too; a TENSOR_REDUCE from SBUF beside it took its usual 0.68. Beside a GpSimd MEMSET of 128x1280, which reads nothing, the plain form took 0.81 and ended with it, and SCALAR_TENSOR_TENSOR took 0.17 (first tile, changed kernel and run 4). The Trainium skill has this rule ("SBUF — State Buffer", section "Who interferes with whom"): the plain tensor_scalar may use the port pair shared with GpSimd, two inputs from SBUF need the read side of that pair, and reductions and the accumulator form need none of it. All four forms agree with it here.
- The accumulator of an activation is read by an instruction of its own of 0.2 us, of which 0.093 shows from start to start (0.393 with it, 0.300 without, 128x77 from PSUM with two pointer operands).
- PE's idle time alone did not tell when its clock would fall: 1.88 and 2.28 us in one batch of run 4, and 1.95 in run 9, left it at 1.00 in those batches, while 1.96 was followed by 0.50 in the changed kernel. In run 12 an idle of 1.96 left it at 1.00 in one batch (window from 161 to 167), and one of 1.95 in a later batch was followed by 0.64 (window from 197 to 201). A half clock costs only where PE is the one waited for: some 3 us in the first tiles of the changed kernel, at most 0.2 a batch behind them, 0.4 to 1 us in three batches of run 9, and 1.6 in a batch of run 8.
